# Row statistics of the first stage's layer norm off VectorE, and the gated delta work of GpSimd respaced

## The reference, cut to what matters

```python
m = x.mean(-1); v = x.var(-1); xn = (x - m) / sqrt(v + 1e-5)
x_, z = split(xn @ in_proj_w.T)
u = silu(causal_conv4(x_) + conv_b)
dt, B, C = split(u @ x_proj_w.T)                 # 64, 16, 16
delta = softplus(dt @ dt_proj_w.T + dt_proj_b)   # [rows, 512]
h = exp(delta * A) * h + (delta * u) * B         # a state of 512 x 16 per sequence, row after row
y = (h * C).sum(states) + u * D
s = (y * silu(z)) @ out_proj_w.T
```

## Time and profile before

| what | us |
|---|---|
| median of 3 runs (lowest, highest) | 5582.43 (5580.23, 5583.1) |
| the profiled execution, its own time | 5581.44 |
| its span, first to last instruction | 5579.8 |
| first stage, up to the last gate product on VectorE | 1875 |
| busy in the span: PE, DVE, ACT, POOL | 4915.1, 4199.2, 3014.7, 2928.8 |

### The profile page before, as it was taken

One profiled execution on the slowest core, in us unless ns is written; L12 is line 12 of the kernel. 1 busy time (PEld: TensorE's weight loads), 2 busy tenths in 40 slices (PEclk: granted clock), 3 DMA queues, 4 the chain that ended last, 5 costly groups with the idle time before them and its releaser, 6 DMA issues. The chain is left out here.

```text
span 5579.8 us, 79659 instructions
## 1 busy us (share of the span) xinstructions
PE 4915.1 (88%) x26068; PEld 2908.6 (52%) x26068; DVE 4199.2 (75%) x8641; ACT 3014.7 (54%) x6489; POOL 2928.8 (52%) x1603
## 2 busy tenths in 40 slices
PE   6787778877886599999999999999999999998886
PEld 2233233323332377777555566666665555665765
DVE  3999999999999799999533377777763337996259
ACT  5776877777776477777311255555541113553232
POOL 4899989998999556565210244444431010002742
PEclk9898889888987699999999999999999999999997
DMA  5665566556655232323112111111111134444768
GB/s 133 152 152 142 138 154 153 142 138 154 153 139 129 70 92 84 92 85 116 39 57 59 56 35 35 36 38 35 46 45 57 55 111 136 143 143 133 195 146 178
DMA packets 493022, 585.40 MB, mean 105 GB/s; under 512 B 59446, under 2 KB 372548, under 8 KB 488516
## 3 DMA queue, kind: packets, MB, share of 16 engines
q1 hardware_dynamic: 461412, 554.19, 36.7%
q0 software_dynamic: 29184, 18.78, 2.3%
q10 hardware_dynamic: 2016, 7.34, 0.4%
HBM read 416.67 MB, written 180.37 MB: 107 GB/s over the span
## 5 line engine op out<-in xcount | busy, mean ns | idle before, releaser
L692 POOL TENSOR_TENSOR db<-durep,brep 128x2048 f32<-128x2048 f32 x256 | 1160.0, 4531 | 114.5 <-DVE p_h L597 103.3
L536 ACT ACTIVATE p_h<-dlrep,am 128x512 f32<-128x512 f32 x1024 | 701.5, 690 | 177.8 <-DVE hh L608 152.5
L597 DVE TENSOR_TENSOR_SCAN p_h<-p_h,hlast,db 128x512 f32<-128x512 f32 x576 | 717.8, 1277 | 11.3 <-ACT hlast L525 9.9
L1309 POOL TENSOR_TENSOR rot_cos<-rot_cos,rot_sin 128x1024 f32<-128x1024 f32 x128 | 302.2, 2361 | 536.4 <-DVE rot_sin L1230 536.4
L608 DVE TENSOR_TENSOR hh<-p_h,crep 128x512 f32<-128x512 f32 x768 | 515.4, 671 | 0.0
L1305 POOL TENSOR_TENSOR rn<-n,mhalf 128x16 f32<-128x16 f32 x128 | 374.9, 2929 | 265.5 <-DVE n L1240 265.4
L352 PE MATMUL p_acc<-hh,fold 128*32 128x512 f32 x2048 | 310.4, 682 | 219.4 <-DVE hh L608 218.1
L1672 POOL TENSOR_TENSOR grstd<-grstd,mhalf 128x4 f32<-128x4 f32 x32 | 32.6, 1018 | 728.4 <-DVE grstd L1589 728.2
L987 PE MATMUL p_s<-qkT 64*128 64x128 f32 x4096 | 299.6, 286 | 76.4 <-DVE nb L1195 75.3
L1574 ACT ACTIVATE gg<-p_s,b 128x512 f32<-128x512 f32 x160 | 109.9, 687 | 447.3 <-PE p_o L1517 265.8
L1098 ACT ACTIVATE probB<-probB,nb 128x256 f32<-128x256 f32 x512 | 254.3, 499 | 163.9 <-DVE nb L1195 163.9
(11 more groups left out here) (291 smaller groups left out, 11773.9 us busy)
## 6 DMA issues: line engine op xcount, KB each, us to landing
dlrep<-delta_rows SPq DMA_DIRECT2D x256, 256.0 KB
durep<-drive_rows SPq DMA_DIRECT2D x256, 256.0 KB
ew<-in_L_ffn_w SPq DMA_DIRECT2D x192, 176.0 KB
first_queries_keys<-qs SPq DMA_DIRECT2D x128, 256.0 KB, 2.1
qk<-first_queries_keys SPq DMA_DIRECT2D x64, 512.0 KB, 3.9
brep<-bc_rows SPq DMA_DIRECT2D x64, 256.0 KB
crep<-bc_rows SPq DMA_DIRECT2D x64, 256.0 KB
delta_rows<-dl SPq DMA_DIRECT2D x64, 256.0 KB
```

What stands on the lines that cost most here:

```text
L536: act.activation(p_h[:, (i % BANKS) * CH:(i % BANKS + 1) * CH], dlrep[use % 2][:, j], ACT.Exp, scale=am[:, q, j, g:g + 1]).then_inc(s_ex, 1)
L597: dve.tensor_tensor_scan(out=state, data0=bank, data1=db[s % 2][:, j], initial=0.0 if first else hlast[:, i % TILES:i % TILES + 1], op0=AL ...
L692: pool.tensor_tensor(out=db[s % 2][:], in0=durep[use % 2][:], in1=brep[c % 2][:, g:g + 1, :].to_broadcast([P, 4, CH]), op=ALU.mult).then_i ...
L1309: pool.tensor_tensor(out=rc[:], in0=rc[:], in1=rsn[:], op=ALU.add).then_inc(s_rot, 1)
```

## The change

- `negative_mean` on VectorE is gone, and with it the tile `nsum`. ScalarE's `sums` becomes `negative_means`: the same four activations with a scale of -1/256, so that the accumulator gives the negative mean straight into `nnb`. The activation's full output goes to the space of `dl[:, 0:2]` rather than in place, so the two waits for the stores of those quarters move here from `square_sums`, which now waits for ScalarE's own sums.
- `variance` moves from VectorE (behind step 7) to GpSimd, directly ahead of `rstd` in its step 8.
- GpSimd's eight `delta` and `weighted` move from steps 0, 2, 4, 6, 9, 10, 12, 14 to steps 1, 3, 5, 7, 9, 11, 13, 15.
- SP's list is reordered to suit: `store_qk(c + 1, 0)` ahead of `store_delta(c, 2)`; `spread_bc(c + 1)` and `store_qk(c + 1, 1)` ahead of `store_delta(c, 3)`; `store_delta(c + 1, 0)` behind `store_qk` 3 and `store_out(c - 1, 0)`, and `store_qk` 4 ahead of `spread_delta(c + 1, 0)`; `store_delta(c + 1, 1)` last.

```diff
--- before.py
+++ after.py
@@ -178,7 +178,7 @@
     hs = [sb(f"hs{k}", [P, CH]) for k in range(2)]
     hlast = sb("hlast", [P, TILES])
     so = sb("so", [P, 2, D])
-    nsum, nsq = sb("nsum", [P, CT]), sb("nsq", [P, CT])
+    nsq = sb("nsq", [P, CT])
     squares_at = dl[:, 0:2].rearrange("p q t -> p (q t)").rearrange("p (j d) -> p j d", d=D)
     p_h = ps("p_h", BANKS * CH)
     p_acc = ps("p_acc", CH)
@@ -190,8 +190,8 @@
     s_dw = [sem(f"m_dw{q}") for q in range(Q)]
     s_one, s_aexp, s_aneg, s_skipw, s_fold, s_taps = (
         sem("m_" + n) for n in ("one", "aexp", "aneg", "skipw", "fold", "taps"))
-    s_nst, s_nmv, s_nva, s_nrs, s_nnb, s_nrm, s_sum, s_nm, s_sq = (
-        sem("m_" + n) for n in ("nst", "nmv", "nva", "nrs", "nnb", "nrm", "sum", "nm", "sq"))
+    s_nst, s_nmv, s_nva, s_nrs, s_nnb, s_nrm, s_sum, s_sq = (
+        sem("m_" + n) for n in ("nst", "nmv", "nva", "nrs", "nnb", "nrm", "sum", "sq"))
     s_tr, s_inx, s_inz, s_xp, s_dt, s_ac, s_op = (sem("m_" + n) for n in ("tr", "inx", "inz", "xp", "dt", "ac", "op"))
     s_xT, s_xr, s_zr, s_u, s_sz, s_xd, s_rl, s_ea, s_ln, s_hl, s_ex, s_so = (
         sem("m_" + n) for n in ("xT", "xr", "zr", "u", "sz", "xd", "rl", "ea", "ln", "hl", "ex", "so"))
@@ -370,16 +370,16 @@
 
         @block.scalar
         def _(act):
-            def sums(f):
+            def negative_means(f):
                 act.wait_ge(s_x, 16 * (f + 1))
-                for j in range(CT):
-                    ins = act.activation(xin[:, j], xin[:, j], ACT.Copy, accum_out=nsum[:, j:j + 1])
-                ins.then_inc(s_sum, 1)
-
-            def square_sums(f):
-                act.wait_ge(s_nm, f - 1)
                 for q in range(2):
                     act.wait_ge(s_dw[q], 32 * (f - 1))
+                for j in range(CT):
+                    ins = act.activation(squares_at[:, j], xin[:, j], ACT.Copy, scale=-1.0 / D, accum_out=nnb[:, j:j + 1])
+                ins.then_inc(s_sum, 1)
+
+            def square_sums(f):
+                act.wait_ge(s_sum, f - 1)
                 for j in range(CT):
                     ins = act.activation(squares_at[:, j], xin[:, j], ACT.Square, bias=nnb[:, j:j + 1], accum_out=nsq[:, j:j + 1])
                 ins.then_inc(s_sq, 1)
@@ -477,7 +477,7 @@
                 if n in (10, 12) and c > 0:
                     out_proj(c - 1, (n - 10) // 2)
                 if n == 4 and 0 <= c < NC - 2:
-                    sums(c + 2)
+                    negative_means(c + 2)
                 if n == 11 and c + 2 < NC:
                     norm(c + 2)
                 f = c + 2 if n > 14 else c + 1
@@ -559,14 +559,6 @@
 
         @block.vector
         def _(dve):
-            def negative_mean(c):
-                dve.wait_ge(s_sum, c - 1)
-                dve.tensor_scalar(nnb[:], nsum[:], -1.0 / D, None, ALU.mult).then_inc(s_nm, 1)
-
-            def variance(c):
-                dve.wait_ge(s_sq, c - 1)
-                dve.tensor_scalar(nrs[:], nsq[:], 1.0 / D, 1e-5, ALU.mult, ALU.add).then_inc(s_nva, 1)
-
             def stats(c):
                 dve.wait_ge(s_x, 16 * (c + 1))
                 for j in range(CT):
@@ -640,14 +632,14 @@
                         use = c * Q + n // NG
                         if n % NG == 0 and j == 1 and use > 0:
                             gate((use - 1) // Q, (use - 1) % Q)
-                    if n == 5 and c + 2 < NC:
-                        negative_mean(c + 2)
-                    if n == 7 and c + 2 < NC:
-                        variance(c + 2)
             gate(NC - 1, Q - 1)
 
         @block.gpsimd
         def _(pool):
+            def variance(c):
+                pool.wait_ge(s_sq, c - 1)
+                pool.tensor_scalar(nrs[:], nsq[:], 1.0 / D, 1e-5, ALU.mult, ALU.add).then_inc(s_nva, 1)
+
             def rstd(c):
                 pool.wait_ge(s_nva, c + 1)
                 pool.tensor_tensor(out=nrs[:], in0=nrs[:], in1=mhalf[:, 0:CT], op=ALU.pow).then_inc(s_nrs, 1)
@@ -708,15 +700,16 @@
                     if n == 6 and c + 2 < NC:
                         carry(c + 2)
                     if n == 8 and c + 2 < NC:
+                        variance(c + 2)
                         rstd(c + 2)
-                    if n in (9, 12) and c + 1 < NC:
-                        delta(c + 1, n // 12)
-                    if n in (10, 14) and c + 1 < NC:
-                        weighted(c + 1, n // 14)
-                    if n in (0, 4) and c > 0:
-                        delta(c, 2 + n // 4)
-                    if n in (2, 6) and c > 0:
-                        weighted(c, 2 + n // 6)
+                    if n in (9, 13) and c + 1 < NC:
+                        delta(c + 1, n // 13)
+                    if n in (11, 15) and c + 1 < NC:
+                        weighted(c + 1, n // 15)
+                    if n in (1, 5) and c > 0:
+                        delta(c, 2 + n // 5)
+                    if n in (3, 7) and c > 0:
+                        weighted(c, 2 + n // 7)
             weigh(NC * STEPS - 1)
 
         @block.sync
@@ -807,26 +800,26 @@
                 spread_delta(c, 1)
                 if c + 2 < NC:
                     load_x(c + 2)
+                if c + 1 < NC:
+                    store_qk(c + 1, 0)
                 if c > 0:
                     store_delta(c, 2)
-                if c + 1 < NC:
-                    store_qk(c + 1, 0)
                 spread_delta(c, 2)
-                if c > 0:
-                    store_delta(c, 3)
                 if c + 1 < NC:
                     spread_bc(c + 1)
                     store_qk(c + 1, 1)
+                if c > 0:
+                    store_delta(c, 3)
                 spread_delta(c, 3)
                 if c + 1 < NC:
                     store_qk(c + 1, 2)
-                    store_delta(c + 1, 0)
                     store_qk(c + 1, 3)
                 if c > 0:
                     store_out(c - 1, 0)
                 if c + 1 < NC:
+                    store_delta(c + 1, 0)
+                    store_qk(c + 1, 4)
                     spread_delta(c + 1, 0)
-                    store_qk(c + 1, 4)
                 if c + 2 < NC:
                     store_xn(c + 2)
                 if c + 1 < NC:
@@ -835,8 +828,8 @@
                     store_out(c - 1, 1)
                 if c + 1 < NC:
                     store_qk(c + 1, 6)
+                    store_qk(c + 1, 7)
                     store_delta(c + 1, 1)
-                    store_qk(c + 1, 7)
             store_out(NC - 1, 0)
             store_out(NC - 1, 1)
             sp.wait_ge(s_sxn, 16 * NC)
```

More of the change, by code:

```diff
@@ L372, in _ @@
         def _(act):
-            def sums(f):
+            def negative_means(f):
                 act.wait_ge(s_x, 16 * (f + 1))
+                for q in range(2):
+                    act.wait_ge(s_dw[q], 32 * (f - 1))
                 for j in range(CT):
-                    ins = act.activation(xin[:, j], xin[:, j], ACT.Copy, accum_out=nsum[:, j:j + 1])
+                    ins = act.activation(squares_at[:, j], xin[:, j], ACT.Copy, scale=-1.0 / D, accum_out=nnb[:, j:j + 1])
                 ins.then_inc(s_sum, 1)
             def square_sums(f):
-                act.wait_ge(s_nm, f - 1)
-                for q in range(2):
-                    act.wait_ge(s_dw[q], 32 * (f - 1))
+                act.wait_ge(s_sum, f - 1)
                 for j in range(CT):
```

## The result

| | before | after |
|---|---|---|
| median of 4 runs (lowest, highest), us | 5582.15 (5580.23, 5583.1) | 5540.58 (5535.94, 5542.7) |
| the profiled execution's own time, us | 5581.44 | 5540.01 |
| its span, us | 5579.8 | 5538.4 |
| last gate product of the first stage on VectorE, starts at | 1875.19 | 1829.85 |
| mean granted TensorE clock | 0.941 | 0.942 |

The ratio is 0.9924, with the interval 0.9912 to 0.9935: 41.6 us less on the medians, 41.4 us on the profiled executions. The forecast was 50 us less and the range (5520 to 5550) held the time; what has to be explained is the 8 us that did not come, and whether the 42 came for the reasons given.

A forecast was written before the change was run, and what follows sets the result against it. VectorE was taken to bound the first stage, some 1875 us of the 5580. The terms 24.7 + 1.0 + 20.4 + 4.2 = 50.3 us less gave a forecast of 5532 us, range 5520 to 5550.

The forecast's parts named there:

- The stall of L564, net 24.7 us: VectorE, first stage, step 6: removing L564 saves 39.6 us over 14 chunks, less 14.9 us of exposed waits for ScalarE.
- ScalarE's lateness in step 6: First stage, step 6: scans wait for ScalarE's silus and table loads, formerly hidden by L564; 14.9 us in sum.
- L568, the 42 waits and their overlap, 25.6 us: VectorE, first stage: L568 leaving saves 1.0 us, 42 scan waits for GpSimd's drive 20.4, overlap of neighbours 4.2.
- The rival in which another engine holds VectorE anyway: First stage: whole 2.83 us stall exposed or drive waits staying, about 25 us remain, 5557 us; chance 0.04.
- The variance on GpSimd, 0.2 us: GpSimd, step 8: the 128x4 variance instruction costs 0.2 us, inside GpSimd's possible lead of 2.0 us.
- The rival of a dear variance: GpSimd, first stage: at 6 us an instruction 56 us would go, 5588 us, no change; chance 0.02.
- With added products in odd steps only, it is never two steps behind: GpSimd, first stage: with spaced products its 2.0 us lead suffices, so the 20.4 us of drive waits go.
- Quarter 3, 28.1 us from B and C to usable data: SP's queue, first stage: the later du store still lands before drive 12; cost 0, spare 0.2 to 1.5 us.
- its own sign of being wrong: First stage: drive 12 released by a DMA, or db waits in steps 12 and 13, would disprove quarter 3's timing.
- ScalarE's new form, 0 to 0.4 us a chunk, taken as 0: ScalarE, step 5: the scaled copy lies between 401 and 496 ns, in a place where nothing waits.
- The square sums in step 7: ScalarE, step 7: decay behind them fits by 0.1 us; 0 to 0.5 us a chunk may be lost, taken as 0.
- check on the pair: Chunks 13 and 14, kernel before: durations differ by 3.30 us, terms give 3.16; difference put down to overlap, 4.2 us.

The follow-up runs named there:

- experiment 4: Kernel before with only GpSimd's products moved to odd steps and SP's new order; L564 and the variance stay on VectorE: 5571.97 us.
- experiment 8: Kernel before with GpSimd's power (rstd) one step later, in step 9: 5585.39 us, ratio 1.0006.
- experiment 3: Kernel before with the whole statistics change (mean to ScalarE, variance to GpSimd), GpSimd's products and SP's order as before: 5536.49 us.
- experiment 7: Changed kernel plus filler matmuls that nobody reads, placed where TensorE would wait: 5530.18 us.
- experiment 9: Kernel before with the whole statistics change, old spacing and SP order, plus filler matmuls in TensorE's waits: 5528.95 us.
- experiment 6: Statistics change with old spacing and SP order, plus TensorE's step 15 state sums put ahead of the next chunk's input projections: 5550.05 us.
- experiment 12: Changed kernel measured once more, nothing altered: 5538.91 us, ratio 0.992.

## Why the prediction was right, and where it was short

**The stall of L564, net 24.7 us: right.** Step 6 won 24.2 us in the changed kernel, and 24.2 or 24.3 in every other run without L564. ScalarE's lateness in step 6 is the wait of 1.10 us shown above. What I had seen of the stall was its size; experiments 4 and 8 show its cause. The same 128x4 operation takes 0.15 us beside an idle GpSimd and 2.4 to 2.9 us beside a drive of 4.53 us, and ends with the drive. The Trainium skill, page "SBUF — State Buffer", section "Who interferes with whom", says that VectorE's tensor_scalar can take the pair of ports it shares with GpSimd, and that whoever issues first has the pair for its whole instruction while the other is blocked. The traces agree with the blocking (0.02 to 0.03 us from the drive's end to the end of the blocked instruction); no run here shows the ports.

**L568, the 42 waits and their overlap, 25.6 us: right in sum, 1.1 us too much.** Steps 8 to 10 won 24.5 us; the 4.2 us put down for overlap were somewhat high. The 0.9 us of step 12 do not belong here: they are the gate's wait for TensorE in chunk 0, and they also came with the mean alone and with the fillers alone. The rival in which another engine holds VectorE anyway (5557) falls: no `db` wait took the place of the old ones.

**The variance on GpSimd, 0.2 us: right.** It took 194 ns. The rival of a dear variance falls with it: all 14 took 194 or 195 ns, with 1.2 us of idle time ahead of them in all, so the 6 us that the Trainium skill, page "GPSIMD Engine Reference", section "Instruction dispatch", gives for a first call of freshly loaded code were not paid here.

**"With added products in odd steps only, it is never two steps behind": true and without effect.** I gave the respacing no term of its own but let the 20.4 us rest on it. Experiment 3 has none of it and no drive waits but one of 0.2 us. Once GpSimd does not stop ahead of the power, two added products in a row fit into its lead. The respacing pays only where the stop stays (experiment 4).

**Quarter 3, 28.1 us from B and C to usable data: right in the number and the cost, though its own sign of being wrong came.** The queue of SP in chunk 14, with B and C's store, the `du` store and the spread:

```profile
1660.10 0.32 SPq L740 DMA_DIRECT2D bc_rows<-xd  x1
...
1668.21 0.44 SPq L756 DMA_DIRECT2D drive_rows<-du  x1
1675.71 1.76 SPq L766 DMA_DIRECT2D dlrep<-delta_rows  x4
```

and the drive that needs the quarter, in GpSimd's timeline:

```profile
1688.14 4.54 POOL L684 TENSOR_TENSOR db<-durep,brep 128x2048 f32<-128x2048 f32 x1 [0.56 <-DMA durep<-drive_rows]
```

The spread goes out 15.6 us behind B and C (16 forecast), and the data is usable 1688.14 - 1660.10 = 28.04 us behind them. I had said that no drive would be released by a transfer inside the loop, and that a drive 12 so released would prove the step wrong. Four were, all of them drive 12 (in chunks 3, 11, 12 and 14, by 1.3 us in all); GpSimd's lead took it and no scan waited: in chunk 14 the scan of step 12 starts at 1693.98, 1.30 us behind the drive's end, with 1.5 forecast. The sign was set too sharply. The `du` store to the spread took 7.5 us. The 2.6 us that I had worked out for such a transfer from the Trainium skill, page "DMA: Bandwidth & Descriptors", section "Anatomy of one DMA — SWDGE (gpsimd) path", are an estimate from a fit for transfers issued by GpSimd, and these are SP's, behind 2 MB of others: the start-up's row was the one to trust.

**ScalarE's new form, 0 to 0.4 us a chunk, taken as 0: right.** The scaled copies (L378) take the 401 ns of the old sums. **The square sums in step 7, "fits by 0.1 us": right only at TensorE's full clock.** With the fillers step 7 lasts 6.50 us. In the changed kernel `x_proj` ran longer in some chunks; TensorE's timeline in chunk 7:

```profile
891.32 6.66 PE L258 MATMUL p_f<-uu,w_xp 128*96 128x512 f32 x8 [2.85 <-ACT uu L437]
```

It was 5.04 us there in the kernel before; the granted clock during these matmuls was 0.55, and 0.72 in the kernel before. ScalarE's copy of its result comes later, then the decay, and a scan of step 7 waits 0.42 us. That is the 2.5 us of step 7, of a spread that I had put at up to 7.

**The step that failed** is the tacit one that chunk 14's pace, with its gate waits, holds for every chunk of the new kernel. My check on the pair promised 109.3 us for chunk 13. Chunks 5 and 9, of the same kind, did last 109.35 and 109.34; chunk 13 lasted 110.65. The argument had VectorE, ScalarE, GpSimd and the transfers in it, and no term for TensorE, since its gate waits were already in the kernel before and I let them stand as a constant. They are not one. TensorE waits for ScalarE shortly before the input projection and before `x_proj`, its clock drops around there, and how much of these two stretches runs at 1.2 GHz depends on where they come relative to the drop. That a faster VectorE is what moves them is my reading of the traces: the losses differ from program to program, and no run sets the moment of a drop by itself. In sum over the chunks this cost 1.7 us in step 0 and 2.5 in step 7 here, 10.3 and 3.1 with the mean alone, and 3.5 in step 0 with the variance alone or the respacing alone. With the clock held, the forecast of 50.3 us compares with 47.5 (experiment 7) and 48.7 (experiment 9), both against the kernel before with the same fillers.

**The sum of the shortfall** on the profiled executions, 50.3 - 41.4 = 8.9 us: 4.3 us in steps 0 and 7, 3.9 us that came back behind the first stage, 1.6 us in the terms (24.7 against 24.2; 25.6 against 24.5) and 0.2 us in step 11. Against that stand 0.9 us won in step 12 and 0.4 us at the start, which no term had. What is left is rounding. The 3.9 us are argued from the two traces alone. They shrink in pieces: the gain is 45.3 us at the last gate product, 43.4 at the last rotation (rot_cos, which starts at 4083.8 instead of 4127.2) and 41.4 at the end of the span. The stretch behind the last gate product was longer than in the one trace of the kernel before in all the other traces, by 0.8 us (the mean alone) to 5.4 (experiment 6), and also where the change is absent: by 2.7 us with the fillers alone and about 1.2 in experiment 8. So these 3.9 us (4.2 in experiment 12) need not come from the change at all. Whether they are TensorE's clock in the later stages or scatter of the one trace they are compared with wasn't tried and stays open.

**What wins.** The kernel of experiment 9, the statistics change without the respacing and with TensorE's waits filled, is at 5528.95 us the fastest of all, 11.6 us under the changed kernel. It can't be told from experiment 7.

## What to carry to other kernels

When a stall leaves the bounding engine, its own price is easy to read off; what the new pace does to the others is not, and a wait that was there before is not a constant, because the moment at which TensorE's clock drops can move against the work that others wait for. So list every wait of the bounding engine that an engine with a changing clock ends, give each a low and a high price by rows at either level, or hold the clock up with matmuls in TensorE's waits, and measure the parts of a change against that version, where its drops no longer hide what a part is worth. And a tiny VectorE instruction that takes microseconds should be read together with what GpSimd is doing at that moment, before any work is moved that keeps GpSimd idle there.

## What the runs showed that I had not expected

- Extra matmuls that nobody reads made the kernel faster: by 10.4 us on the changed kernel and 7.5 us on that of experiment 3, but only 4.8 on the kernel before, where the interval reaches no change.
- The same eight projection matmuls took 3.70, 5.48 and 6.78 us, at granted clocks of 1.00, 0.62 and 0.51 in the windows around them. TensorE was not the bound, and still each microsecond beyond the gate's slack was VectorE's.
- A 128x4 tensor_scalar on VectorE costs between 0.15 and 2.92 us, by what GpSimd runs beside it. Where it is long, it starts inside a drive and ends with it. Removing GpSimd's wait (experiment 8) moved 31 us of stall onto VectorE's L568 and won nothing in sum.
- Two parts worth 11 and 21 us alone were worth 45.5 us together.
